# Diffusion attention: turned sums, last maxima, a tile of q and half an output projection one step down; input statistics and a turned tile up

## The reference, cut to what matters

```python
def _token_diffusion(x, Wqk, Wv, Wo, tau):          # 16 heads of 16
    qk = (x @ Wqk) by heads;  v = (x @ Wv) by heads
    logits = (2 qk qk^T - |q|^2 - |k|^2) / 4 * tau
    return softmax(logits) @ v, heads joined, @ Wo
def _channel_diffusion(...):                         # 8 heads of 32 channels, the same over channels
x = x + _token_diffusion(_layernorm(x, ...)) * gamma1
x = x + _channel_diffusion(_layernorm(x, ...)) * gamma2
```

## Time and profile before

| | |
|---|---|
| median of 3 runs | 4381.61 us (4377.87 to 4384.84) |
| profiled execution, its own time | 4382.84 us |
| span of its profile | 4381.0 us |
| busy over the span | PE 85%, DVE 55%, ACT 40%, POOL 37% |
| mean granted TensorE clock | 0.924 |
| first scores of diffusion attention | 2883.9 us |
| passes 1 to 6 | 104.9, 106.3, 106.0, 106.2, 106.2, 107.9 us |
| pass 7 and start of the drain, to the last exponential | 117.9 us |

### The profile page before, as it was taken

The page is one execution under the profiler, slowest core; times in us unless marked ns, Lnnn a source line. Parts: engine busy times, 40 slices in busy tenths (PEclk is TensorE's granted clock), DMA queues, the critical chain, the costliest instruction groups (busy, mean ns, idle before and its releaser), DMA issues. The chain is left out here.

```text
span 4381.0 us, 64166 instructions
## 1 busy us (share of the span) xinstructions
PE 3709.8 (85%) x17520; PEld 2209.8 (50%) x17584; DVE 2415.1 (55%) x6529; ACT 1752.6 (40%) x4010; POOL 1619.3 (37%) x1750
## 2 busy tenths in 40 slices
PE   6999999999689998997999899679999998459940
PEld 3555555566345555554555555335555554346630
DVE  6766676677465662224656433245566665345556
ACT  2544444455345554112555511035555545114420
POOL 2333333333466762004667512401222221352244
PEclk8999999999799999999999999879999999669975
DMA  6555665557201112443011211132222221249952
GB/s 103 71 74 68 84 84 79 71 65 92 67 25 39 48 43 99 158 164 105 34 38 48 74 46 60 41 79 53 61 56 54 54 50 47 89 166 312 312 169 70
DMA packets 230366, 378.28 MB, mean 86 GB/s; under 512 B 39822, under 2 KB 166099, under 8 KB 223699
## 3 DMA queue, kind: packets, MB, share of 16 engines
q1 hardware_dynamic: 216658, 355.13, 34.4%
q0 software_dynamic: 6144, 16.79, 1.2%
q10 hardware_dynamic: 7296, 3.22, 0.3%
HBM read 170.03 MB, written 84.93 MB: 58 GB/s over the span
## 5 line engine op out<-in xcount | busy, mean ns | idle before, releaser
L758 DVE CUSTOM_DVE_ANT_0 a_ps<-a_ps,a_mask 128x128 f32<-128x128 f32 (+3 forms) x1024 | 481.0, 513 | 219.1 <-PE a_ps L513 199.6
L2618 DVE TENSOR_REDUCE c_neg_max<-c_ps 128x1 f32<-128x512 f32 x512 | 340.8, 684 | 244.5 <-PE c_ps L2286 243.1
L2479 ACT ACTIVATE c_probsT<-c_ps 128x512 f32<-128x512 f32 x512 | 299.2, 598 | 400.1 <-PE c_ps L2298 391.2
L368 POOL TENSOR_SCALAR_AFFINE_SELECT a_probs_c<-a_probs_c 128x256 f32<-128x256 f32 (+1 forms) x384 | 185.8, 500 | 699.5 <-ACT a_probs_c L663 699.2
L663 ACT ACTIVATE a_probs_c<-a_ps 128x512 f32<-128x512 f32 x640 | 344.6, 603 | 119.5 <-PE a_ps L531 84.4
L513 PE MATMUL a_ps<-a_packed_qk 65*128 65x128 f32 (+3 forms) x1024 | 336.9, 373 | 53.5 <-DVE a_maxima L758 28.0
L1094 POOL TENSOR_TENSOR w_probs<-w_probs,w_inv 128x1024 f32<-128x1024 f32 x128 | 242.3, 1893 | 334.8 <-DVE w_inv L1457 334.8
L549 PE MATMUL a_ps<-a_probs_c,a_v 128*64 128x512 f32 (+3 forms) x2048 | 329.9, 468 | 1.8 <-POOL a_probs_c L368 0.8
L531 PE MATMUL a_ps<-a_packed_qk 67*128 67x512 f32 (+3 forms) x1024 | 288.8, 345 | 0.8 <-DMA a_packed_qk<-a_max_half 0.8
L2286 PE MATMUL c_ps<-c_packed_qk 68*128 68x512 f32 x512 | 263.2, 519 | 4.4 <-DVE c_neg_max L2618 2.2
L1349 ACT ACTIVATE w_probs<-w_ps_s,w_neg_max 128x256 f32<-128x256 f32 x512 | 236.0, 478 | 68.2 <-DVE w_neg_max L1452 66.9
(11 more groups left out here) (323 smaller groups left out, 7805.9 us busy)
## 6 DMA issues: line engine op xcount, KB each, us to landing
a_packed_qk<-a_halves SPq DMA_DIRECT2D x512, 128.0 KB, 4.6
d_w<-in_L_ffn_second SPq DMA_DIRECT2D x71, 516.0 KB, 5.0
d_w<-in_L_ffn_first SPq DMA_DIRECT2D x71, 512.0 KB, 5.1
rows_dram<-f_zeros SPq DMA_DIRECT2D x8, 4096.0 KB, 16.1
c_packed_qk<-c_halves SPq DMA_DIRECT2D x256, 128.0 KB, 2.4
w_v<-w_v_next SPq DMA_DIRECT2D x16, 1024.0 KB, 4.7
d_rows<-rows_dram SPq DMA_DIRECT2D x71, 128.0 KB, 4.3
mixed_dram<-d_y SPq DMA_DIRECT2D x71, 128.0 KB, 4.9
```

The lines of the kernel that those rows point to most:

```text
L758: last = nc.vector.tensor_tensor_reduce(tile, tile, mask[:, (NT - 1 - i) * P:], 1.0, -3e38, ALU.add, ALU.max, accum_out=maxima_of[:, hd // ...
L2479: nc.scalar.activation(probsT[:, q % 2, r, :], ps_again[u % 2][:, :], ACT.Exp).then_inc(exp_done.sem, 1)
L2618: nc.vector.tensor_reduce(neg_max[:, g % 2, 0, s % GS:s % GS + 1], bank("s", s)[:, :], AX.X, ALU.max, negate=True).then_inc(max_ready.sem, 1)
```

## The change

In step numbers of the tables, PE does last maxima (m3) after step 1 and not 0, the fourth tile of q (q3) after 7 and not 6, the turned sums t2, t3, t0 and t1 after 10, 26, 42 and 58 and not 9, 25, 41 and 57 (t3 behind v3, t0 behind c1). The second turned input tile (h1) and the second half of the output projection (y1) change places: h1 after 30, y1 after 31. ACT and DVE follow. The DVE's low half of m3 goes before maxima 3, the combines go one step down, and the second half's statistics (a1) go after maxima 33. The input statistics (i) go from after maxima 15 to 18 to after 10 to 13. On ACT, the squares and halves of q3 now stand in step 8 right behind the copy of the sums s2, and its keys in step 9. `combine` also waits for its own previous result.

```diff
--- before.py
+++ after.py
@@ -1826,29 +1826,29 @@
 
 
 
-    EXTRA = {0: [("m", 3, -1)], 2: [("q", 2, 0)], 6: [("q", 3, 0)], 9: [("t", 2, -1)], 11: [("v", 2, 0)],
-             12: [("n", 1, 0)], 13: [("o", 0, -1)], 16: [("m", 0, 0)], 25: [("t", 3, -1)], 26: [("v", 3, 0)],
-             27: [("o", 1, -1)], 28: [("h", 0, 1)], 29: [("y", 0, -1)], 30: [("y", 1, -1)], 31: [("h", 1, 1)],
+    EXTRA = {1: [("m", 3, -1)], 2: [("q", 2, 0)], 7: [("q", 3, 0)], 10: [("t", 2, -1)], 11: [("v", 2, 0)],
+             12: [("n", 1, 0)], 13: [("o", 0, -1)], 16: [("m", 0, 0)], 26: [("v", 3, 0), ("t", 3, -1)],
+             27: [("o", 1, -1)], 28: [("h", 0, 1)], 29: [("y", 0, -1)], 30: [("h", 1, 1)], 31: [("y", 1, -1)],
              32: [("m", 1, 0)], 33: [("q", 0, 1)], 37: [("g", 0, -1)], 38: [("g", 1, -1)], 39: [("q", 1, 1)],
-             40: [("c", 0, -1)], 41: [("t", 0, 0)], 42: [("c", 1, -1)], 44: [("r", 0, -1)], 45: [("w", 0, -1)],
+             40: [("c", 0, -1)], 42: [("c", 1, -1), ("t", 0, 0)], 44: [("r", 0, -1)], 45: [("w", 0, -1)],
              46: [("d", 0, -1)], 47: [("w", 1, -1)], 48: [("m", 2, 0)], 50: [("n", 0, 1)], 51: [("x", 0, -1)],
-             52: [("v", 0, 1)], 53: [("z", 0, -1)], 54: [("z", 1, -1)], 57: [("t", 1, 0)], 60: [("v", 1, 1)]}
-
-
-    AFTER_EXP = {1: [("m", 3, -1)], 3: [("q", 2, 0)], 4: [("k", 2, 0)], 7: [("q", 3, 0)], 8: [("s", 2, -1), ("k", 3, 0)],
-                 12: [("v", 2, 0)], 13: [("n", 1, 0)], 14: [("o", 0, -1)], 17: [("m", 0, 0)], 24: [("s", 3, -1)],
-                 27: [("v", 3, 0)], 28: [("o", 1, -1)], 29: [("h", 0, 1)], 32: [("h", 1, 1)], 33: [("m", 1, 0)],
-                 34: [("q", 0, 1)], 35: [("k", 0, 1)], 38: [("g", 0, -1)], 39: [("g", 1, -1)], 40: [("s", 0, 0)],
-                 41: [("c", 0, -1), ("q", 1, 1)], 42: [("k", 1, 1)], 43: [("c", 1, -1)], 46: [("w", 0, -1)],
-                 48: [("w", 1, -1), ("e", 0, -1)], 49: [("m", 2, 0)], 51: [("n", 0, 1)], 52: [("x", 0, -1)],
-                 53: [("v", 0, 1)], 56: [("s", 1, 0)], 61: [("v", 1, 1)]}
-
-
-    BEFORE_MAX = {2: [("m", 3, -1)], 10: [("t", 2, -1)], 18: [("m", 0, 0)], 26: [("t", 3, -1)], 30: [("y", 0, -1)],
-                  31: [("y", 1, -1)], 34: [("m", 1, 0)], 42: [("t", 0, 0)], 45: [("r", 0, -1)], 47: [("l", 0, -1)],
-                  50: [("m", 2, 0), ("f", 0, -1)], 54: [("z", 0, -1)], 55: [("z", 1, -1)], 58: [("t", 1, 0)]}
-    AFTER_MAX = {5: [("q", 2, 0)], 9: [("q", 3, 0)], 14: [("n", 1, 0)], 15: [("i", 0, 1)], 16: [("i", 1, 1)],
-                 17: [("i", 2, 1)], 18: [("i", 3, 1)], 31: [("a", 0, -1)], 32: [("a", 1, -1)], 36: [("q", 0, 1)],
+             52: [("v", 0, 1)], 53: [("z", 0, -1)], 54: [("z", 1, -1)], 58: [("t", 1, 0)], 60: [("v", 1, 1)]}
+
+
+    AFTER_EXP = {2: [("m", 3, -1)], 3: [("q", 2, 0)], 4: [("k", 2, 0)], 8: [("s", 2, -1), ("q", 3, 0)],
+                 9: [("k", 3, 0)], 12: [("v", 2, 0)], 13: [("n", 1, 0)], 14: [("o", 0, -1)], 17: [("m", 0, 0)],
+                 24: [("s", 3, -1)], 27: [("v", 3, 0)], 28: [("o", 1, -1)], 29: [("h", 0, 1)], 31: [("h", 1, 1)],
+                 33: [("m", 1, 0)], 34: [("q", 0, 1)], 35: [("k", 0, 1)], 38: [("g", 0, -1)], 39: [("g", 1, -1)],
+                 40: [("s", 0, 0)], 41: [("c", 0, -1), ("q", 1, 1)], 42: [("k", 1, 1)], 43: [("c", 1, -1)],
+                 46: [("w", 0, -1)], 48: [("w", 1, -1), ("e", 0, -1)], 49: [("m", 2, 0)], 51: [("n", 0, 1)],
+                 52: [("x", 0, -1)], 53: [("v", 0, 1)], 56: [("s", 1, 0)], 61: [("v", 1, 1)]}
+
+
+    BEFORE_MAX = {3: [("m", 3, -1)], 11: [("t", 2, -1)], 18: [("m", 0, 0)], 27: [("t", 3, -1)], 30: [("y", 0, -1)],
+                  32: [("y", 1, -1)], 34: [("m", 1, 0)], 43: [("t", 0, 0)], 45: [("r", 0, -1)], 47: [("l", 0, -1)],
+                  50: [("m", 2, 0), ("f", 0, -1)], 54: [("z", 0, -1)], 55: [("z", 1, -1)], 59: [("t", 1, 0)]}
+    AFTER_MAX = {5: [("q", 2, 0)], 10: [("q", 3, 0), ("i", 0, 1)], 11: [("i", 1, 1)], 12: [("i", 2, 1)],
+                 13: [("i", 3, 1)], 14: [("n", 1, 0)], 31: [("a", 0, -1)], 33: [("a", 1, -1)], 36: [("q", 0, 1)],
                  43: [("q", 1, 1)], 52: [("n", 0, 1)], 55: [("b", 0, -1)], 56: [("b", 1, -1)]}
 
 
@@ -2633,6 +2633,8 @@
 
             def combine(b, g):
                 dve.wait_ge(sums_psum.sem, sums_psum.at(b, g + 1))
+                if g:
+                    dve.wait_ge(o_ready.sem, o_ready.at(b, g))
                 heads = bank("t", g)[:, :].rearrange("p (t r d) -> p t r d", t=NT, d=ROWS)
                 nc.vector.reciprocal(inv[:, :, :], heads[:, :, :, DH]).then_inc(inverted.sem, 1)
                 dve.wait_ge(inverted.sem, inverted.at(b, g + 1))
```

## The result

| | before | after |
|---|---|---|
| median | 4381.56 us (4 runs, 4377.87 to 4384.84) | 4409.82 us (4 runs, 4398.44 to 4411.71) |
| ratio, 95% interval | | 1.0052 (1.0033 to 1.0072) |
| span of the profiled execution | 4381.0 us | 4396.5 us |
| mean granted clock | 0.924 | 0.913 |
| passes 1 to 6 | 104.9, 106.3, 106.0, 106.2, 106.2, 107.9 us | 102.8, 108.8, 103.2, 115.6, 108.8, 103.3 us |

The prediction was 4360 us and faster. Slower had a chance of 0.08, with the clock as its mechanism. The profiled execution is the fastest of the four, so its trace shows only part of the loss; the other three have a lower mean clock (0.910 and 0.911).

What follows compares the result with a forecast made beforehand. PE was taken as the bound, busy 97.6 of 106.2 us in pass 5, with waits and half-clock stretches to gain. Terms summed to -21.3 us from 4382.84, giving 4361.5, then 4360 as median; 8-in-10 range 4347 to 4377.

Steps and rivals of the forecast that it cites:

- The clock: Half-speed stretches behind PE's longer waits: four behind steps 0 and 6 go, those behind g0 stay; -6.8 us.
- The term of -6.8 us: Four stretches of 3.4 us at 0.50 in passes 2, 4, 5 and 6 vanish, 1.7 us gained each.
- the slower rival: Waits before g0 and in steps 10 and 11 bring fourteen more low stretches, none of four goes: 4391 us; chance 0.07.
- m3 and its copy: Pass entry: copy L2622 is issued before POOL's add, so m3's 1.39 us wait goes in passes 3 to 7; -7.0 us.
- The +2.1 for a wait in step 6: scores_again of step 6 waits up to 0.3 us for the DMA, as m3's chain is one exponential longer; seven passes.
- q3: Step 7 with its weighing now covers the wait of 1.59 us for DVE's split of q2; -10.7 us over seven passes.
- t2 and the squares: t2's 0.69 us wait goes, but step 11 waits for a later exponential on ACT: moved and grown, +2.4 us.
- t3, t1: Turned sums: t3's 0.78 us wait is covered, -5.5 us; t1 gains 0.47 and keeps 0.3 us, -3.8 us.
- y1 and h1: The swap makes g0 start 1.0 us later in passes 1 to 6, 1.5 in pass 7; +7.5 us.
- Input statistics: Five steps earlier, they keep the gain from becoming a wait for hn; no wait of their own, 0 us.
- c1: Comes 0.3 us earlier, but the channel products behind it wait for the split of q1; nothing gained.
- The sum without the clock: The forecast's terms for waits removed, moved or added on PE, leaving out the clock's -6.8 us.

Runs made afterwards that it cites:

- swap_only: The kernel before with only y1 and h1 (with a1) changed round and combine's added wait; ratio 1.0049, median 4398.4 us.
- u_i: The changed kernel with the input statistics put back behind maxima 15 to 18; ratio 1.0012, median 4382.8 us.
- u_i_q3: The changed kernel with both the input statistics and q3 (with its ACT and DVE parts) put back; ratio 1.0014, median 4390.1 us.
- fill3: The changed kernel, order untouched, with useless matmuls in its waits in steps 11 and 16 and ahead of g0; ratio 0.9944, median 4356.9 us.
- warm_before: The kernel before with two useless matmuls of ident by wqk ahead of g0; ratio 0.9976, median 4376.1 us.
- fill20: The changed kernel with two extra scores matmuls in step 20, where PE does not wait; ratio 1.0099, median 4424.3 us.
- u_swap_i: The changed kernel with y1, h1 and a1 and also the input statistics put back; ratio 1.0007, median 4384.6 us.
- u_swap: The changed kernel with y1, h1 and a1 put back in their old places; ratio 0.9969, median 4375.0 us.

## Why the prediction was wrong, step by step

- **The clock** is the step that failed. The term of -6.8 us, for the four low stretches behind the waits of steps 0 and 6, came as written: all four are gone. What failed is that the sum put nothing for new ones. It counted the wait that moved to step 11 by its length alone, and the argument against the slower rival was that waits of 0.7 and 0.8 us had brought no low stretch. That held for t2, t3 and t1 where they stood. A wait of 0.67 us ahead of a weighing and v2 brought one of 10.2 us in four of seven passes, and m0's wait one of 17.1 us in one. In passes 1 to 6 these are 24 us of lost time (length by half), and 5 more in pass 7. With 1.7 more behind g0 and the -6.8, the time lost in passes 1 to 6 grew from 24 to 43 us. The price of a stretch, taken from 3.4 us, was too low by a factor of 3 to 5. The row that could have warned of it was there: pass 0, with 23.9 us at half clock and PE busy in it, was not looked into. Nor do the passes repeat to a few tenths: they do from 3 to 5, but 1 to 6 range from 104.9 to 107.9 us.
- **m3 and its copy**: right. No wait of L2319 at the entry of a pass, and the copy is issued 0.44 us before the add, where a margin of 0.45 was predicted. The +2.1 for a wait in step 6 did not come. The copy took 0.29 us and not 0.17: it was issued 0.95 us into a TENSOR_SCALAR of 1.22 and ended with it. Here the Trainium skill's rule (SBUF — State Buffer, "Who interferes with whom") was right, that the second to issue is blocked to the end, and my reading of the row at 2973.31 was too wide. It costs nothing, as step 1 hides it. The order did not rest on t1 alone: in swap_only the copy also escapes the add, by 0.01 to 0.02 us.
- **q3**: right, no wait, though scores_again of step 7 waits 0.33 us for an exponential, within the bound.
- **t2 and the squares**: right in place, 0.67 us where 0.9 was expected in step 11. So the wait moved and did not grow. What it does to the clock was given to a rival.
- **t3, t1**: t3 has no wait, as written. t1 has 0.06 us where 0.3 was to stay.
- **y1 and h1**: right. g0 waits 3.42 us, where 3.2 were predicted, and begins 1.05 us later against y0, where 1.0 was predicted.
- **Input statistics** at 0 was wrong. They bring m0's wait of 0.6 us in passes 1 to 6 and, by u_i and u_i_q3, the 17 us stretches. I had named only POOL's small instructions as a danger, not that DVE falls behind in steps 13 to 15.
- **c1**: the wait only moved, to 0.61 us ahead of the channel products, as written.
- **The sum without the clock**: -2.5 us a pass by the terms, in a pass where the copy had been blocked. Pass 3 against pass 3 is 103.2 against 106.0, with the same 6.8 us low in each. But 2.2 us of that stretch fall on g0's wait in the changed kernel, and 0.5 in the one before. PE's idle time (length less PE busy) is the better measure: 6.3 us against 8.5, so -2.2. At the full clock fill3 takes 101.1 us where warm_before's pass 5 takes 103.0, so -1.9. That the sum came so near is in part luck: what t1, t2 and step 6 gave beyond their terms covered most of what m0 and the channel products took. Pass 3 of the kernel before, columns as in rows 1:

```profile
3184.90:3290.90 106.00, 97.47 (x479) 54.82 (x475) 65.12 (x128) 54.05 (x105) 27.68 (x31) 0.97 0.23 56
```

So the waits were read rightly in the main, and the time came out on the other side, by the mechanism that had been given 0.07.

## What to carry to other kernels

When PE is the bound and its granted clock is not 1.00 throughout, a wait has two prices: its own length, and a low stretch behind it, which may be longer than any that the trace before has at such a place. Count the waits that a reordering leaves or makes on PE, not only their sum, and compare passes of one trace: equal instructions with unequal times point to the clock. Where a wait can't be removed, try harmless matmuls in it: two of them in one wait took 0.6% off this kernel, and the same two where PE did not wait added 0.5%. And look where two spans differ before explaining the difference: here 6 of 15.5 us lay in code that nobody had changed.

## What the hardware showed that I had not expected

- PE was busy for all of a stretch of 17.07 us and the granted clock stayed at 0.50 in it. Work alone didn't bring it back at once.
- The same wait of 0.67 us brought a low stretch in four passes of seven in the changed kernel, in six of seven in fill20 and in all seven of u_swap_i, where the passes 1 to 6 had one length and the stretch came at the same place each time. It brought none in five of the seven in u_swap. What decides whether it comes is open.
- The wait of 0.6 us ahead of the channel products brought no low stretch in any of passes 1 to 6, in any kernel that has it. So the length of a wait doesn't tell its price.
- A DVE copy issued 0.54 us into a POOL TENSOR_SCALAR took 0.17 us, one issued 0.95 us into one took 0.29. Over all the traces, the 27 copies issued 0.06 to 0.69 us into a TENSOR_SCALAR of 1.22 took 0.17 to 0.21 us, and the 67 issued 0.93 to 0.96 us into one took 0.29 to 0.33 and ended with it. Why the late part of the instruction blocks and the early part doesn't is open.
- Against the add L2161 (a TENSOR_TENSOR of 2.4 us) a hundredth of a us decides: issued from 0.02 us before the add to together with it, the copy took 0.17 or 0.18 us (eight times, six of them in swap_only), and issued 0.01 to 0.02 us after it, 2.37 or 2.38 (ten times).
